# Deformable sampling on one engine: who makes the products, when the distances come, and how long TensorE runs on zeros

## The chip, the cores and the metric

The kernel runs on one core of one Trainium2 chip. The metric is the device time of one execution in microseconds, and a kernel's time is the median of several executions. A core has five engines that run side by side: TensorE (PE in the profile, with its weight loads as PEld), VectorE (DVE), ScalarE (ACT), GpSimd (POOL) and SyncE (SP), which here only issues transfers. They wait for each other through semaphores.

## The reference, cut to what matters

The input x is (8, 32, 16, 16) in fp32. Three layers follow each other, each added to its input: a deformable 3x3 convolution, a state-space scan of 64 states over 256 tokens, and a chain of 33 attention and feed-forward layers in which the data choose which are carried out. Only the first is touched:

```python
x = x + _L0_conv_ref(_gn(x), offset_w, offset_b, weight, bias)

offsets = conv2d(x, offset_w, offset_b, PAD)            # 18 channels: dy, dx of 9 taps
ys = (arange(H) - PAD) + kh + dy
xs = (arange(W) - PAD) + kw + dx
sampled = bilinear_sample(x, ys, xs)                    # (b, tap, y, x, c)
out = einsum('bkhwc,ock->bohw', sampled, w) + bias
```

Bilinear sampling is a weighted sum over all 256 positions of the image: position (i, j) has the weight max(0, 1 - |ys - i|) * max(0, 1 - |xs - j|).

## The kernel before, in words

**Preparation.** x lies as 128 partitions (4 image pairs times 32 channels) by two halves of 256 positions. VectorE normalises it into a zero-padded tile, xpad (L550), and copies it out unpadded (L555). TensorE computes the offsets with nine shifted fp32 matmuls (L803, two passes each in the trace, 18 records), VectorE adds bias and grid (L561), TensorE turns the result so that positions are partitions (L839). Ahead of the nine matmuls stands `keep_warm(12)` (L828): twelve bf16 matmuls of zeros, 128x512, that nobody reads (L824). Beside this TensorE multiplies the image with the nine taps' weights ("filters", L817) in four parts, and ScalarE copies each part out of PSUM in two instructions (`evacuate_filters`, L391).

**The weights of bilinear sampling.** They are made in six rounds, `it` = 0 to 5: three kernel rows times two halves. `distances(it)` on VectorE writes y or x position minus level (L568) and its absolute value (L573), 768 elements a partition. `hats(it)` on ScalarE makes max(0, 1 - that) of it (L398). Then each of the round's three taps, j = 0, 1, 2, needs a product of its row hat and its column hat, `sampling_chunk` (L228): 2048 elements a partition, fp32, both inputs in SBUF and broadcast. There are 18 such chunks. Tile `samp[j]` is one buffer for each j, so the product of round `it` waits until TensorE has turned the chunk of round it - 1 with the same j (L226). VectorE makes j = 0 and 1, GpSimd makes j = 2.

**What TensorE and ScalarE do with a chunk.** TensorE turns a chunk with 16 transposes (`turn`, L860) in two sides of eight. ScalarE copies each side out of PSUM (L415) into `sampT[j]`. TensorE then adds up the tap with 16 matmuls (`tap_sum`, L870) into a PSUM bank that is kept through all 18 chunks. TensorE's order is written out: turn of chunk n, then tap sum of chunk n - 1 (L876 to L880).

**The order of the queues before.** Every engine works off its list in order.

- VectorE: distances 0 and 1, then for each round products j = 0 and 1, then the distances of round it + 2 (L575 to L582).
- GpSimd: some constants (L323 to L333), then the products j = 2 of rounds 0 to 5 (L337), then it waits for the second layer (L340).
- ScalarE: filters 0 and 1, hats 0, filters 2, hats 1, filters 3 (L400 to L405), then for each round the six copies of the turned sides, with the hats of round it + 2 behind those of j = 1 (L417).
- TensorE: the twelve zero matmuls, the offset matmuls, filters, the turn of the offsets, filters (with four zero matmuls in front of parts 2 and 3), then x itself as a matmul with the identity (L846), a wait for all filters (L847), then the 18 chunks.

Behind the last tap sum VectorE adds the bias (L586) and the next layer begins. The state-space layer (L637, L648 and L362 above all) and the chain of layers (from L1009) are not touched.

Of the kernel before, what the change touches and what calls it, by code (L numbers as in the profile page):

```python
# [14 lines left out]
SIDE = 16  # L15
PAIRS, HALVES = 4, 2
# [26 lines left out]
def hybrid_kernel(nc, x, const, offset_w, conv_w, ssm_w, spread_w, masks, steps, w_attn, w_up, w_down, out):  # L43
# [7 lines left out]
    with ctx:  # L51
# [43 lines left out]
        def region(phase, n):  # L95
            a = used[phase]
            used[phase] = a + n
            assert used[phase] <= 31 * 1024
            return pool[:, a:a + n]
# [9 lines left out]
        samp = [region("conv", 8 * HW).rearrange("p (c n) -> p c n", c=8) for _ in range(3)]  # L109
# [45 lines left out]
        def bank(i, n=1):  # L155
            return ps[:, i * BANK:(i + n) * BANK]
# [10 lines left out]
        def slot(e):  # L167
# [10 lines left out]
        off_done, off_ready, offT_done, hat_diff, hat_ready = map(  # L178
            sem, ["off_done", "off_ready", "offT_done", "hat_diff", "hat_ready"])
        z_done, z_ready = map(sem, ["z_done", "z_ready"])  # L180
        samp_made = [sem(f"samp_made{j}") for j in range(3)]
        samp_turned, turned_ready, chunk_summed, conv_done = map(
            sem, ["samp_turned", "turned_ready", "chunk_summed", "conv_done"])
# [33 lines left out]

        ROWS = 3

        def sampling_chunk(eng, it, j):  # L220

            eng.wait_ge(hat_ready, it + 1)

            if it:

                eng.wait_ge(samp_turned, 6 * (it - 1) + 2 * j + 2)  # L226
            now = hat[:, it, :, 2 * j:2 * j + 2, :]
            eng.tensor_tensor(samp[j].rearrange("p c (y x) -> p c y x", y=SIDE),  # L228
                              now[:, :, 0, :].unsqueeze(3).broadcast_to([128, 8, SIDE, SIDE]),
                              now[:, :, 1, :].unsqueeze(2).broadcast_to([128, 8, SIDE, SIDE]),  # L230
                              ALU.mult).then_inc(samp_made[j], 1)

        def column_half(c):
            return slice(c * BANK, (c + 1) * BANK)
# [31 lines left out]
        def _(sp):  # L266
# [19 lines left out]

            regs = control_registers(sp, "sp")
            steps_done, _, _ = counters(sp, "sp")
            layer, op = regs[0], regs[1]
            sp.wait_ge(ctl_ready, 1)  # L290
# [23 lines left out]
        @block.gpsimd  # L314
        def _(pool_e):
            pool_e.memset(ones[:, :], 1.0).then_inc(table_input, 1)
            pool_e.memset(eps[:, :], GN_EPS).then_inc(eps_set, 1)
            pool_e.memset(zero_bf[:, :], 0.0).then_inc(zero_set, 1)  # L318
            pool_e.memset(xpad, 0.0).then_inc(pad_zeroed, 1)
            pool_e.memset(wbd[:, :, :], 0.0).then_inc(wbd_zeroed, 1)  # L320

            pool_e.wait_ge(spread_in, 16)
            pool_e.tensor_copy(picks[:, :].rearrange("p (j b d) -> p b j d", j=PER, b=HALVES),  # L323
                               spread[:, :].rearrange("p (b j) -> p b j", b=HALVES).unsqueeze(3)
                               .broadcast_to([96, HALVES, PER, DI])).then_inc(picks_ready, 1)

            pool_e.wait_ge(const_in, 16)
            onehot = part["onehot"].rearrange("p (b w) -> p b w", b=HALVES)
            pool_e.tensor_copy(chosen[:, 0:2 * PER - 1], onehot[:, 0, :]).then_inc(chosen_ready, 1)  # L330
            pool_e.tensor_copy(chosen[:, 2 * PER - 1:], onehot[:, 1, PER - 1:]).then_inc(chosen_ready, 1)

            pool_e.tensor_copy(row0_picks[:, :].rearrange("p (k d) -> p k d", k=GROUPS * HALVES),  # L333
                               ident.rearrange("p (k j) -> p k j", j=PER)[:, :, 0].unsqueeze(2)
                               .broadcast_to([128, GROUPS * HALVES, DI])).then_inc(row0_picks_ready, 1)

            for it in range(HALVES * ROWS):  # L337
                sampling_chunk(pool_e, it, 2)

            pool_e.wait_ge(c_ready, 1)  # L340

            def product(e):
                j, g = divmod(e, GROUPS)
                if j >= 2:

                    pool_e.wait_ge(prod_summed, j - 1)
                pool_e.wait_ge(scanned, e + 1)
                return prod[GROUPS * (j % 2) + g], state[e % GROUPS]

            def added(j):  # L350
                e = GROUPS * j + GROUPS - 1
                pool_e.wait_ge(delta_copied, j + 1)
                if j:

                    pool_e.wait_ge(scanned, e - GROUPS + 1)
                pool_e.tensor_tensor(dbx[e % GROUPS], bx, delta_wide[j % 2], ALU.mult).then_inc(pool_dbx_ready, 1)  # L356

            pool_e.wait_ge(bx_ready, 1)
            for e in range(DI - 2):
                j, g = divmod(e, GROUPS)  # L360
                to, of = product(e)
                pool_e.tensor_tensor(to, of, cn, ALU.mult).then_inc(prod_ready, 1)  # L362
                if g == 0 and j < PER - 1:
                    added(j)
            to, of = product(DI - 2)
            for c in range(2):
                pool_e.tensor_tensor(to[:, column_half(c)], of[:, column_half(c)], cn[:, column_half(c)],
                                     ALU.mult).then_inc(late_prod_ready, 1)
# [3 lines left out]
        def _(act):  # L372
# [14 lines left out]
            def evacuate_filters(n):  # L387
                half, side = divmod(n, 2)
                for two in range(2):
                    act.wait_ge(z_done, 2 * n + two + 1)  # L390
                    act.activation(zs[:, half, 2 * two:2 * two + 2, side, :], bank(3 + 2 * two, 2)  # L391
                                   .rearrange("p (q k) -> p q k", q=2)[:, :, 0:TAPS * C], ACT.Copy).then_inc(z_ready, 1)

            def hats(i):

                act.wait_ge(hat_abs, i + 1)
                v = hat[:, i, :, :, :].rearrange("p c o y -> p (c o y)")
                act.activation(v, v, ACT.Relu, bias=1.0, scale=-1.0).then_inc(hat_ready, 1)  # L398
# [2 lines left out]
            evacuate_filters(1)  # L401
            hats(0)
            evacuate_filters(2)
            hats(1)
            evacuate_filters(3)  # L405

            for it in range(HALVES * ROWS):
                for j in range(3):
                    if it:

                        act.wait_ge(chunk_summed, 3 * (it - 1) + j + 1)
                    for side in range(2):
                        s = 2 * j + side
                        act.wait_ge(samp_turned, 6 * it + s + 1)
                        act.activation(sampT[j][:, 2 * side:2 * side + 2].rearrange("p q h n -> p (q h n)"),  # L415
                                       bank(2 + 2 * (s % 3), 2), ACT.Copy).then_inc(turned_ready, 1)
                    if j == 1 and it + HALVES < HALVES * ROWS:  # L417
                        hats(it + HALVES)

            def layer_norm(n):
# [30 lines left out]
            for e in range(DI):  # L452
                j, g = divmod(e, GROUPS)
# [72 lines left out]
        def _(dve):  # L526
# [37 lines left out]
            def distances(i):  # L564
                kk, half = divmod(i, HALVES)
                pos = bank(1)[:, half * HW:(half + 1) * HW].rearrange("p (c o) -> p c o", c=8)[:, :, 6 * kk:6 * kk + 6]
                v = hat[:, i, :, :, :]
                dve.tensor_tensor(v, pos.unsqueeze(3).broadcast_to([128, 8, 6, SIDE]),  # L568
                                  part["level"].unsqueeze(1).unsqueeze(1).broadcast_to([128, 8, 6, SIDE]),
                                  ALU.subtract).then_inc(hat_diff, 1)  # L570
                dve.wait_ge(hat_diff, i + 1)
                flat = v.rearrange("p c o y -> p (c o y)")
                dve.scalar_tensor_tensor(flat, flat, -1.0, flat, ALU.mult, ALU.max).then_inc(hat_abs, 1)  # L573

            dve.wait_ge(offT_done, 1)  # L575
            for half in range(HALVES):
                distances(half)
            for it in range(HALVES * ROWS):
                for j in range(2):
                    sampling_chunk(dve, it, j)  # L580
                if it + HALVES < HALVES * ROWS:
                    distances(it + HALVES)  # L582

            dve.wait_ge(conv_done, 1)
# [209 lines left out]
        def _(pe):  # L795
# [25 lines left out]
            def keep_warm(n, at=7):  # L821

                for _ in range(n):
                    pe.matmul(bank(at), zero_bf[:, 0:128], zero_bf[:, :], start=True, stop=True)  # L824

            pe.wait_ge(zero_set, 1)
            keep_warm(12)  # L828
            pe.wait_ge(offw_in, 16)
            pe.wait_ge(xn_ready, HALVES)  # L830
            offset_taps(range(TAPS)).then_inc(off_done, 1)
# [135 lines left out]
            for e in range(DI):  # L967
                spread_delta(e)
                j, g = divmod(e, GROUPS)
# [244 lines left out]
```

## Time and profile before

| | us |
|---|---|
| median of three executions | 369.01 (368.79 to 369.76) |
| the profiled execution | 367.8, its span 366.0 |
| PE busy | 261.8 (72% of the span) |
| DVE busy | 283.0 (77%) |
| ACT busy | 165.2 (45%) |
| POOL busy | 209.7 (57%) |

The span runs from the first to the last instruction; all times inside it are counted from its start. The times in the table are sums over stages with different limits, so the reading below goes by stage.
### The profile page before, as it was taken

What the parts mean: (1) busy time and instruction counts of PE and PEld (TensorE: products, weight loads), DVE (VectorE), ACT (ScalarE), POOL (GpSimd) and SP (SyncE); (2) the same over time, 40 slices, a digit from 0 to 9 for tenths busy, and PEclk for the clock granted to TensorE, in tenths of its full rate; (3) what the DMA queues carried; (4) which work ended last, traced back from release to release, by engine and by line L of the source; (5) the groups of instructions that cost most, each with busy time, mean ns of one, the idle gap of its engine ahead of it and who ended that gap; (6) DMA issues with size and microseconds to landing.
All of it is one profiled execution on the core that took longest, in us unless ns stands there. A gap on an engine that the chain in (4) does not pass through costs nothing. (4 is left out here: it accounts for less than half of the span.)

```text
span 366.0 us, 3919 instructions
## 1 busy us (share of the span) xinstructions
PE 261.8 (72%) x1382; PEld 99.2 (27%) x1388; DVE 283.0 (77%) x223; ACT 165.2 (45%) x263; POOL 209.7 (57%) x98
## 2 busy tenths in 40 slices
PE   5996999997852765477557745775576587788983
PEld 1435777773420000000000000000000143235630
DVE  1179999703589999999999999999999993123731
ACT  1063777662653444344434443444344350334431
POOL 2231444440039999999999999999999850000000
PEclk9898999999996655655565565555565599999999
DMA  6100000000120000000000000000000000000000
GB/s 202 56 0 2 2 0 2 2 3 0 29 58 2 0 0 0 0 1 2 0 0 0 1 0 1 2 0 0 0 0 0 0 2 0 13 18 0 0 0 29
DMA packets 2498, 3.88 MB, mean 11 GB/s; under 512 B 687, under 2 KB 1712, under 8 KB 2480
## 3 DMA queue, kind: packets, MB, share of 16 engines
q1 hardware_dynamic: 2216, 3.45, 3.3%
q8 instruction: 11, 0.18, 0.2%
q10 hardware_dynamic: 264, 0.20, 0.2%
q14 instruction: 7, 0.06, 0.1%
HBM read 2.59 MB, written 0.26 MB: 8 GB/s over the span
## 5 line engine op out<-in xcount | busy, mean ns | idle before, releaser
L362 POOL TENSOR_TENSOR pool<-pool 128x1024 f32<-128x1024 f32 x62 | 144.7, 2355 | 39.3 <-DVE pool L648 39.3
L648 DVE TENSOR_TENSOR_SCAN pool<-ps,pool 128x1024 f32<-128x1024 f32 x63 | 143.8, 2283 | 0.6 <-ACT ps L464 0.5
L957 PE MATMUL ps<-pool,picks 96*128 96x512 bf16 x120 | 59.1, 593 | 72.9 <-DVE pool L648 72.9
L462 ACT ACTIVATE ps<-ps,ssmw 128x1020 f32<-128x1020 f32 x64 | 69.4, 1084 | 74.3 <-DVE pool L637 74.3
L963 PE MATMUL ps<-pool,chosen 128*32 128x512 f32 x256 | 59.4, 1022 | 1.8 <-DVE pool L665 1.8
L637 DVE TENSOR_TENSOR pool<-pool,ps 128x1024 f32<-128x1024 f32 x49 | 58.5, 1195 | 0.8 <-PE ps L938 0.8
L957 PEld LDWEIGHTS ps<-pool,picks 96*128 96x128 bf16 x120 | 7.7, 108 | 146.1 <-DVE pool L648 146.1
L228 POOL TENSOR_TENSOR pool<-pool 128x2048 f32<-128x2048 f32 x6 | 23.6, 3928 | 38.4 <-PE ps L860 29.8
L415 ACT ACTIVATE pool<-ps 128x1024 f32<-128x1024 f32 x36 | 34.9, 1023 | 18.6 <-PE ps L860 18.6
L860 PE MATMUL ps<-cst,pool 128*128 128x128 f32 x288 | 36.5, 282 | 3.8 <-DVE pool L228 3.8
L860 PEld LDWEIGHTS ps<-cst,pool 128*128 128x128 f32 x288 | 32.5, 144 | 11.1 <-issue 11.1
L356 POOL TENSOR_TENSOR pool<-pool 128x1024 f32<-128x1024 f32 x15 | 35.2, 2346 | 0.2 <-ACT pool L450 0.2
L228 DVE TENSOR_TENSOR pool<-pool 128x2048 f32<-128x2048 f32 x12 | 31.3, 2650 | 2.5 <-PE ps L860 2.5
L450 ACT ACTIVATE pool<-ps 128x1024 f32<-128x1024 f32 x15 | 15.4, 1024 | 32.4 <-PE ps L957 29.6
L824 PE MATMUL ps<-zero_bf 128*128 128x512 bf16 x101 | 26.7, 408 | 2.4 <-POOL zero_bf L318 1.4
L870 PE MATMUL ps<-pool 128*32 128x256 f32 x288 | 19.3, 385 | 0.2 <-ACT pool L415 0.2
L824 PEld LDWEIGHTS ps<-zero_bf 128*128 128x128 bf16 x105 | 10.1, 104 | 18.0 <-issue 8.7
L963 PEld LDWEIGHTS ps<-pool,chosen 128*32 128x32 f32 x256 | 6.6, 140 | 28.6 <-issue 27.0
L573 DVE SCALAR_TENSOR_TENSOR pool<-pool 128x768 f32<-128x768 f32 x6 | 13.2, 2208 | 0.2
L803 PE MATMUL ps<-pool,offw 128*128 128x512 f32 x18 | 9.5, 688 | 3.5 <-DVE pool L550 3.5
L464 ACT ACTIVATE ps<-zero_bf 128x4 f32<-128x4 bf16 x64 | 11.2, 175 | 0.0
L497 ACT ACTIVATE pool<-ps,pool 128x256 f32<-128x256 f32 x16 | 7.4, 479 | 6.6 <-DVE pool L751 6.6
(133 smaller groups left out, 196.4 us busy)
## 6 DMA issues: line engine op xcount, KB each, us to landing
ssmw<-ssm_w_dram SPq DMA_DIRECT2D x1, 896.0 KB, 8.8
pool<-pool SPq DMA_DIRECT2D x12, 64.0 KB, 2.0
offw<-offset_w_dram SPq DMA_DIRECT2D x1, 576.0 KB, 6.6
cst<-const_dram SPq DMA_DIRECT2D x1, 426.0 KB, 7.2
xq<-x_dram SPq DMA_DIRECT2D x2, 128.0 KB
convw<-conv_w_dram SPq DMA_DIRECT2D x1, 144.0 KB, 7.1
pool<-w_up_dram SPq DMA_DIRECT2D x2, 64.5 KB
out_dram<-fin SPq DMA_DIRECT2D x1, 128.0 KB
```

The lines of the kernel that those rows point to most:

```text
L228: eng.tensor_tensor(samp[j].rearrange("p c (y x) -> p c y x", y=SIDE), now[:, :, 0, :].unsqueeze(3).broadcast_to([128, 8, SIDE, SIDE]), no ...
L356: pool_e.tensor_tensor(dbx[e % GROUPS], bx, delta_wide[j % 2], ALU.mult).then_inc(pool_dbx_ready, 1)
L362: pool_e.tensor_tensor(to, of, cn, ALU.mult).then_inc(prod_ready, 1)
L415: act.activation(sampT[j][:, 2 * side:2 * side + 2].rearrange("p q h n -> p (q h n)"), bank(2 + 2 * (s % 3), 2), ACT.Copy).then_inc(turned ...
L462: act.activation(decay[:, :, 1:HW], decay[:, :, 1:HW], ACT.Exp, scale=wt["a"][:, PER * g + j:PER * g + j + 1]).then_inc(da_ready, 1)
L637: dve.tensor_tensor(dbx[e % GROUPS], bx, slot(e), ALU.mult).then_inc(dbx_ready, 1)
L648: dve.tensor_tensor_scan(state[e % GROUPS], slot(e), dbx[e % GROUPS], 0.0, ALU.mult, ALU.add)\
L824: pe.matmul(bank(at), zero_bf[:, 0:128], zero_bf[:, :], start=True, stop=True)
L860: ins = pe.transpose(bank(2 + 2 * (s % 3), 2)[:, at:at + 128], samp[j][:, 4 * t + 2 * side + q, hh * 128:hh * 128 + 128], ident)
L870: ins = pe.matmul(bank(0)[quad(q), half * HW:(half + 1) * HW], zs[:, half, q, hh, k * C:(k + 1) * C], sampT[j][:, q, hh, :], start=False, ...
L957: ins = pe.matmul(slot(e)[:, column_half(c)], picks[:, j * 128:(j + 1) * 128], stack[0:96, g * SEQ + c * BANK:g * SEQ + (c + 1) * BANK], s ...
L963: ins = pe.matmul(bank(c)[quad(g), :], chosen[:, PER - 1 - j:3 * PER - 1 - j], prod[GROUPS * (j % 2) + g][:, column_half(c)], start=False, ...
```

## The change

The changed kernel lets VectorE make all three products of each round, and GpSimd none; the distances of round it + 1 are made behind the first product of round `it`, those of round 0 alone before the first product; ScalarE takes hats 1 behind filters 3, and the hats of round it + 1 behind the copies of chunk j = 0 of round `it`; and the first run of zero matmuls has 20 in place of 12.

```diff
-            for it in range(HALVES * ROWS):
-                sampling_chunk(pool_e, it, 2)
-
             pool_e.wait_ge(c_ready, 1)
...
             hats(0)
             evacuate_filters(2)
+            evacuate_filters(3)
             hats(1)
-            evacuate_filters(3)
...
-                    if j == 1 and it + HALVES < HALVES * ROWS:
-                        hats(it + HALVES)
+                    if j == 0 and 0 < it < HALVES * ROWS - 1:
+                        hats(it + 1)
...
             dve.wait_ge(offT_done, 1)
-            for half in range(HALVES):
-                distances(half)
+            distances(0)
             for it in range(HALVES * ROWS):
-                for j in range(2):
+                for j in range(3):
                     sampling_chunk(dve, it, j)
-                if it + HALVES < HALVES * ROWS:
-                    distances(it + HALVES)
+                    if j == 0 and it + 1 < HALVES * ROWS:
+                        distances(it + 1)
...
             pe.wait_ge(zero_set, 1)
-            keep_warm(12)
+            keep_warm(20)
             pe.wait_ge(offw_in, 16)
```

## Rows read from the trace of the kernel before

**Rows 1.** Stretches: length, busy time of PE, PEld, DVE, ACT, POOL, granted clock, DMA.
```profile
6.40:9.80 3.40, 0.14 (x1) 0.00 (x0) 1.82 (x7) 0.30 (x1) 0.00 (x0) 0.98 1.03 371
9.80:13.10 3.30, 3.07 (x4) 1.51 (x5) 0.52 (x2) 0.00 (x0) 0.49 (x1) 0.50 0.20 78
13.10:30.40 17.30, 13.50 (x60) 5.61 (x59) 9.96 (x6) 6.23 (x10) 6.68 (x5) 0.99 0.00 0
30.40:33.80 3.40, 3.04 (x16) 3.08 (x17) 3.37 (x4) 1.03 (x1) 0.00 (x0) 0.53 0.02 5
33.80:84.80 51.00, 50.48 (x563) 37.08 (x562) 36.91 (x17) 36.82 (x39) 19.13 (x5) 1.00 0.01 1
102.00:311.00 209.00, 130.29 (x453) 22.45 (x452) 201.97 (x127) 92.54 (x149) 181.60 (x79) 0.61 0.01 2
...
```

**Rows 2.** Timeline 0 to 20: start, duration, engine, line, what, count, idle before and releaser.
```profile
1.39 5.15 PE L824 MATMUL ps<-zero_bf 128*128 128x512 bf16 x12 [1.39 <-POOL zero_bf L318]
...
10.03 9.48 PE L803 MATMUL ps<-pool,offw 128*128 128x512 f32 x18 [3.49 <-DVE pool L550]
...
11.87 0.34 PEld L803 LDWEIGHTS ps<-pool,offw 128*128 128x128 f32 x1 [0.52 <-issue]
...
12.72 0.34 PEld L803 LDWEIGHTS ps<-pool,offw 128*128 128x128 f32 x1 [0.52 <-issue]
...
18.07 0.19 PEld L803 LDWEIGHTS ps<-pool,offw 128*128 128x128 f32 x1 [0.24 <-issue]
...
18.50 0.19 PEld L803 LDWEIGHTS ps<-pool,offw 128*128 128x128 f32 x1 [0.24 <-issue]
...
19.56 0.75 DVE L561 SCALAR_TENSOR_TENSOR pool<-ps,cst 128x512 f32<-128x512 f32 x1 [9.21 <-PE ps L803]
```

**Rows 3.** Timeline 20 to 37: distances, hats, first products, first turns.
```profile
23.10 0.84 ACT L398 ACTIVATE pool<-pool 128x768 f32<-128x768 f32 x1
...
24.03 4.43 POOL L228 TENSOR_TENSOR pool<-pool 128x2048 f32<-128x2048 f32 x1 [8.68 <-ACT pool L398]
...
24.85 7.96 DVE L228 TENSOR_TENSOR pool<-pool 128x2048 f32<-128x2048 f32 x2
...
25.76 1.19 ACT L391 ACTIVATE pool<-ps 128x576 f32<-128x576 f32 x2
...
25.88 1.12 PE L846 MATMUL ps<-xq,cst 128*128 128x512 f32 x2
...
30.75 5.05 PE L860 MATMUL ps<-cst,pool 128*128 128x128 f32 x32 [3.75 <-DVE pool L228]
...
32.73 0.94 DVE L568 TENSOR_TENSOR pool<-ps,cst 128x768 f32<-128x768 f32 x1
...
34.59 4.49 DVE L228 TENSOR_TENSOR pool<-pool 128x2048 f32<-128x2048 f32 x2
```

**Rows 4.** Timeline 36 to 85: one round of the even pace, and its end.
```profile
39.64 1.97 PE L860 MATMUL ps<-cst,pool 128*128 128x128 f32 x16
...
42.54 1.97 PE L860 MATMUL ps<-cst,pool 128*128 128x128 f32 x16
...
80.24 1.97 PE L860 MATMUL ps<-cst,pool 128*128 128x128 f32 x16
...
84.85 0.75 DVE L586 TENSOR_SCALAR t<-ps,cst 128x512 f32<-128x512 f32 x1 [11.59 <-remote]
```

**Rows 5.** Line L228: count, shortest, median and longest in ns, first and last start.
```profile
L228 DVE TENSOR_TENSOR pool<-pool x12: 2277/2278/5761, 24.8 to 71.0; 128x2048 f32<-128x2048 f32 x12
```

**Rows 6.** Timeline 293 to 314: the gate's matmuls and their copy, and ten zeros.
```profile
293.67 3.72 PE L920 MATMUL ps<-tn,ssmw 128*128 128x256 f32 x16
...
297.43 1.02 ACT L467 ACTIVATE pool<-ps 128x1024 f32<-128x1024 f32 x1 [0.79 <-PE ps L920]
...
300.06 0.68 DVE L671 TENSOR_TENSOR pool<-ps,pool 128x512 f32<-128x512 f32 x1
...
313.44 2.32 PE L824 MATMUL ps<-zero_bf 128*128 128x512 bf16 x10 [0.54 <-issue]
```

More of the change, by code:

```diff
@@ L218, in hybrid_kernel, with sampling_chunk @@
         ROWS = 3
-        def sampling_chunk(eng, it, j):
-            eng.wait_ge(hat_ready, it + 1)
+        def sampling_chunk(dve, it, j):
+            dve.wait_ge(hat_ready, it + 1)
             if it:
-                eng.wait_ge(samp_turned, 6 * (it - 1) + 2 * j + 2)
+                dve.wait_ge(samp_turned, 6 * (it - 1) + 2 * j + 2)
             now = hat[:, it, :, 2 * j:2 * j + 2, :]
-            eng.tensor_tensor(samp[j].rearrange("p c (y x) -> p c y x", y=SIDE),
+            dve.tensor_tensor(samp[j].rearrange("p c (y x) -> p c y x", y=SIDE),
                               now[:, :, 0, :].unsqueeze(3).broadcast_to([128, 8, SIDE, SIDE]),
```

## The prediction

> **What bounds the kernel now.** I read the busy time by stretches first, then the timeline from 0 to 85, then the waits of line L228, and the two later stages only to see that nothing there is touched. Up to 84.8 the first layer runs; 209 us of state-space scan follow, in which VectorE is busy for 201.97 [rows 1], and then the chain of layers. Neither is changed. What the change does to the time it must do before 84.8, and what it gains there the rest should pass on: the later stages wait for the layer before, not for a transfer.
>
> In the first layer three pieces differ. Up to 10.03 TensorE waits for the padded input. Its offset matmuls then hold everything up for 9.48 us, and VectorE's L561 is waiting for them [rows 2]. From 20 to 31 the first products are on the path: TensorE stands still for 3.75 us for a product of VectorE [rows 3]. From 36.7 on TensorE is the bound: turns start every 2.90 us (39.64, 42.54, ... 80.24), and over 33.8 to 84.8 it is busy for 50.48 of 51.00 us, where VectorE has 36.91 and ScalarE 36.82 [rows 1, 4]. So a faster producer gains nothing in the even pace. A gain can only come from an earlier start of that pace, and a loss only from a producer that falls behind 3 x 2.90 = 8.70 us a round.
>
> **Eight more zeros.** The twelve zeros take 5.15 us, 0.43 each; ten in the last stage take 2.32, 0.23 each [rows 2, 6]. So the first twelve ran at 1.2 GHz (the records of the clock only begin at 6.43). The records then show 2.4 GHz in 6.4 to 9.8, a stretch in which TensorE did 0.14 us of work, and 1.2 GHz in 9.8 to 13.1, just when the offset matmuls start [rows 1]. The engine had worked for 5.15 us when the clock rose and had been idle for 3.3 when it fell. At 1.2 GHz the weight loads of L803 are 0.85 apart (11.87, 12.72), later 0.43 (18.07, 18.50) [rows 2]. With zeros until the input is there the clock should be at 2.4 GHz throughout: 18 x 0.43 = 7.74 instead of 9.48, a gain of 1.7 us. Can eight more zeros be late? At least 8 x 0.23 = 1.9 us, at most 8 x 0.43 = 3.4 are added to the end at 6.54: they end between 8.4 and 9.96, and the offset matmuls start at 10.03. Either way not late; I take the early end, as the clock rose as the twelfth ended, and at worst the hand-over costs 0.1.
>
> The early end leaves TensorE idle for 1.6 us. The Trainium skill (TensorE: Matmul & The Clock Gate, "What's actually happening") lets the clock fall only after a stretch without work, so by it the 1.7 us are safe. The trace is less kind: in the scan TensorE is busy for 130 of 209 us, yet the mean grant is 0.61 [rows 1]. Both ends therefore stand: 0 if the clock falls before the offset matmuls in spite of the zeros, 1.7 if not. I take 1.7: an idle time of 1.6 us is nearer to the short pauses of 13.1 to 30.4 (busy for 13.50 of 17.30, grant 0.99) than to the 3.3 us of nothing after which it fell.
>
> **One distance first, and no GpSimd product.** I work in the times of before and take the 1.7 off at the end. Hats 0 end at 23.94; GpSimd's first product starts at 24.03, VectorE's only at 24.85, behind distances 1. VectorE's first lasts 5.76 us [rows 3, 5], while GpSimd works until 28.46; alone a product lasts 2.28, and two take 34.59 to 38.99, 2.20 apiece. (38.99 is where distances of the next round start; 4.49 is the printed busy time.) 5.76 less the wait until 28.46 (3.61) leaves 2.15: the product waited for GpSimd's to end.
>
> After the change, in VectorE's order: product 0 from 24.0 to 26.2; distances 1, which take 1.86 (32.73 to 34.59 [rows 3]), to 28.1; product 1 to 30.3; product 2 to 32.5. GpSimd's removed products leave nothing behind: its next wait is far later.
>
> ScalarE: filters 3 are copied one hats instruction (0.84) earlier at best, 25.4 to 26.6; hats 1 then wait for distances 1 and run from 28.1 to 28.95. The copies of the first turned chunk are queued behind this wait. The first turn can start at 27.0, when L846 ends [rows 3], so its first side is ready at 28 and waits 1 us; copies of both sides end at 30.9. Who waits for them is the tap sum of chunk 0, which comes behind the turn of chunk 1 (30.35 to 32.3). So that wait is covered by 1.4 us. Tap sum 0 runs to 33.3, and turn 2, whose product was ready at 32.5, starts at 33.3. Before, the turns 0 and 1 ran 30.75 to 35.8 at 1.2 GHz in part (grant 0.53 [rows 1]), a tap sum of 1.0 followed, and turn 2 started at 36.74, which is 15 x 2.90 = 43.5 before the last turn at 80.24 [rows 4]. Gain 36.74 - 33.3 = 3.4 us. It supposes 2.4 GHz in turn 1: idle time before it is 1.35 us in place of 3.75. At 1.2 GHz turn 1 would cost 1 us more.
>
> **The even pace.** VectorE's round is 3 x 2.20 + 1.86 = 8.46, TensorE's is 8.70. Product 4 is ready at 30.3 + 8.46 = 38.8, turn 4 begins at 33.3 + 5.8 = 39.1, and the margin grows by 0.24 a round. The later hats follow the copies of chunk j = 0: turn start + 2.0 + 1.0 + 0.85, some 4.0 us behind the turn; the product and the distances that need them have 8.7 until the next j = 0 turn, so product j = 0 (4.0 + 2.2) is ready 2.5 us early, and product j = 1 (1.86 + 2.2 later) 1.3 us. ScalarE has as many instructions as before. Everything from 36.74 is thus moved as it is.
>
> For this step the Trainium skill offers a rule against the change: Perfetto Trace Analysis, "Optimizing Scalar/DVE Operations", says that offloading to GpSimd may make sense where VectorE is saturated, and adds that between these two it might not help. By the first half the even pace would suffer, and the second rival below is what it would look like.
>
> **The sum.** 1.7 + 3.4 = 5.1, say 5.0 for waits between engines that I have counted as nothing. The profiled execution gives 367.8 - 5.0 = 362.8; it stands 1.2 us under the median of 369.01, which gives 364.0.
>
> **The rivals.**
>
> - *The clock falls before the offset matmuls all the same.* For it: the scan's grant of 0.61 with TensorE busy for 62%. Against: the stretches of rows 1 up to 33.8 as read above. Only 3.4 - 0.1 remain: 365.7. Chance 0.15.
> - *VectorE becomes the bound by a little.* If the products stand 2.28 apart plus 0.1 of handing over each, a round is 3 x 2.38 + 1.96 = 9.1; five rounds of 0.4 more than TensorE's, less the lead of 0.3, cost 1.7: 365.7. For it: a margin of only 0.24 us in 8.7. Against: the pair 34.59 to 38.99, measured with ScalarE and TensorE at work. Chance 0.07.
> - *The clock of the later stages moves.* The gate's matmuls ran at 2.4 GHz in 3.72 us, as the clock rose just before them, and their copy ended at 298.45, where its reader came at 300.06 [rows 6]. With an unlucky clock they take 3.7 more, of which 1.6 are hidden: + 2.1, 366.1. Before and after can both draw this; the three executions lie 1.0 apart. Chance 0.07, and as much of the same size the other way is in the forecast's range.
> - *The product alone is slower than its rows say.* This is the one that ends slower: all 18 lie on VectorE, and were another user of its operands than GpSimd to blame for 5.76, each could cost more than 2.2. Shifted by the 1.7, products start at 22.3, so the last ends at 22.3 + 18p + 5 x 1.86, and the last turn must start no later than 80.24: no gain is left from p = 2.70. At 2.9, between the median and the 5.76, the end is 83.8, so 3.6 later: 372.6. Against it stand the median of 2.28 for twelve and the fit of 5.76 with GpSimd's end. Chance 0.03.
> - *It doesn't start earlier*, say because ScalarE's wait for distances 1 holds back more than I see, and the clock falls too: within 0.3% of before, 369. Chance 0.03.
>
> The forecast itself has 0.65. A difference of about 0.3%, 1.1 us, is what a measurement of this kernel can tell from none. Faster by more: 0.65 + 0.15 + 0.07 + 0.07 = 0.94. The range takes in the first three rivals above, 366.3, and below the case that the executions of before pay more for the clock at 10 and at 31 than the profiled one did (1.7 less): 362.3.
>
> **What would show it.** TensorE: 20 zeros that end by 8.5 to 10; 18 offset matmuls in 7.7 to 7.9 us and the grant at 1.00 over them; L561 near 17.9. VectorE: first product at about 22.3, lasting 2.3; products of 2.20 to 2.28 throughout, GpSimd with none. Turns start every 2.90 from turn 2 at about 31.7; L586 at 79.8 in place of 84.85; scan and chain of layers as long as before. Wrong would be: a grant of 0.5 over L803 (first rival), idle time of TensorE before L860 in later rounds, released by L228 (second or fourth), a tail that is longer than before with the same instructions (third).

## The result and the profile after

The changed kernel takes 363.78 us, the median of four executions (362.57 to 364.62), against 368.9 us before; the ratio is 0.9869 with a 95% interval of 0.9838 to 0.9899. That is 1.3% or some 5 us faster. Of all the executions below five fell in a slower state of the chip (one of the kernel before, two each of two variants), and medians and ratios leave them out. The profiled execution has 363.64 us and a span of 361.9, 4.1 less than before. Lines behind the edits stand three lower in the changed kernel: L857 is the turn, L867 the tap sum, L800 the offset matmuls, L821 the zeros, L583 the bias at the end of the first layer. Turn n and product n are those of chunk n, counted from 0.

The timeline of the changed kernel up to the fourth turn (start, duration, engine, line, what, count, idle before and releaser); it answers to [rows 2] and [rows 3]:

```profile
1.39 7.24 PE L821 MATMUL ps<-zero_bf 128*128 128x512 bf16 x20 [1.39 <-POOL zero_bf L318]
...
10.10 7.97 PE L800 MATMUL ps<-pool,offw 128*128 128x512 f32 x18 [1.47 <-DVE pool L547]
...
18.10 0.75 DVE L558 SCALAR_TENSOR_TENSOR pool<-ps,cst 128x512 f32<-128x512 f32 x1 [7.69 <-PE ps L800]
...
22.52 2.29 DVE L228 TENSOR_TENSOR pool<-pool 128x2048 f32<-128x2048 f32 x1 [0.91 <-ACT pool L395]
...
26.59 6.69 DVE L228 TENSOR_TENSOR pool<-pool 128x2048 f32<-128x2048 f32 x3
26.71 0.84 ACT L395 ACTIVATE pool<-pool 128x768 f32<-128x768 f32 x1 [1.36 <-DVE pool L570]
...
28.94 1.97 PE L857 MATMUL ps<-cst,pool 128*128 128x128 f32 x16 [1.56 <-DVE pool L228]
...
31.84 1.97 PE L857 MATMUL ps<-cst,pool 128*128 128x128 f32 x16
...
37.64 1.73 PEld L857 LDWEIGHTS ps<-cst,pool 128*128 128x128 f32 x16 [0.41 <-DVE pool L228]
```

The 20 zeros end at 8.63, TensorE is idle for 1.47 us, and the offset matmuls take 7.97 us where they took 9.48. The first product lasts 2.29 instead of 5.76. Turn 2 starts at 31.84 (before 36.74). Turns then come every 2.90 us, and turn 4 at 37.64 has its product just in time.

The end of the first layer, answering to [rows 4]:

```profile
75.34 1.97 PE L857 MATMUL ps<-cst,pool 128*128 128x128 f32 x16
...
79.95 0.75 DVE L583 TENSOR_SCALAR t<-ps,cst 128x512 f32<-128x512 f32 x1 [8.40 <-remote]
```

31.84 to 75.34 are the same 43.5 us as 36.74 to 80.24 before. The layer ends 4.90 earlier. The products, in the view of their line, answering to [rows 5]:

```profile
L228 DVE TENSOR_TENSOR pool<-pool x18: 2281/2284/2292, 22.5 to 69.3; 128x2048 f32<-128x2048 f32 x18
```

And the stretches, answering to [rows 1] (length, busy PE, PEld, DVE, ACT, POOL, granted clock, DMA):

```profile
9.80:13.10 3.30, 3.00 (x7) 1.43 (x8) 0.58 (x2) 0.00 (x0) 0.45 (x1) 1.00 0.15 60
...
30.40:80.00 49.60, 48.98 (x549) 35.58 (x548) 41.06 (x25) 35.57 (x38) 0.00 (x0) 1.00 0.01 2
...
97.00:306.00 209.00, 131.31 (x453) 22.94 (x453) 202.07 (x127) 92.47 (x149) 181.51 (x79) 0.60 0.01 3
```

The scan's 209 us are as before. The granted clock stays at 1.00 from the records' first entry to the end of the layer: neither the fall at 9.8 nor the one at 30.4 is there. Of the 4.90 us, 0.75 are given back behind the scan in this execution. The down projection in the first pass of the chain of layers (L1107, at 314.67) takes 3.35 us instead of 2.78, while the clock is at 1.2 GHz (granted clock 0.53 over 314.6 to 317.8), which is 0.57 of them; the rest goes just before it, where TensorE waits for a transfer.

### The profile page after: what moved, and what is told of

Same layout as the page of the kernel before. It is cut to its first block and busy times, and to the rows that moved or that the text cites. A ratio compares the mean times of both kernels' runs of the same rounds, so it can differ in the third digit from the quotient of the medians.

```text
span 361.9 us, 3935 instructions
## 1 busy us (share of the span) xinstructions
PE 262.7 (73%) x1390; PEld 98.7 (27%) x1396; DVE 284.2 (79%) x229; ACT 165.3 (46%) x263; POOL 186.1 (51%) x92
## 3 DMA queue, kind: packets, MB, share of 16 engines
q1 hardware_dynamic: 2216, 3.45, 3.3%
## 5 line engine op out<-in xcount | busy, mean ns | idle before, releaser
L228 DVE TENSOR_TENSOR pool<-pool 128x2048 f32<-128x2048 f32 x18 | 40.1, 2285 | 0.9 <-ACT pool L395 0.9
L857 PE MATMUL ps<-cst,pool 128*128 128x128 f32 x288 | 35.4, 275 | 1.6 <-DVE pool L228 1.6
L857 PEld LDWEIGHTS ps<-cst,pool 128*128 128x128 f32 x288 | 31.2, 140 | 9.1 <-issue 6.2
L821 PE MATMUL ps<-zero_bf 128*128 128x512 bf16 x109 | 28.8, 410 | 2.7 <-POOL zero_bf L318 1.4
L867 PE MATMUL ps<-pool 128*32 128x256 f32 x288 | 19.3, 385 | 0.2 <-ACT pool L412 0.2
L821 PEld LDWEIGHTS ps<-zero_bf 128*128 128x128 bf16 x113 | 11.0, 105 | 20.4 <-issue 10.4
L960 PEld LDWEIGHTS ps<-pool,chosen 128*32 128x32 f32 x256 | 6.7, 140 | 27.6 <-issue 25.9
L388 ACT ACTIVATE pool<-ps 128x576 f32<-128x576 f32 x8 | 4.8, 648 | 10.7 <-PE ps L814 10.7
L867 PEld LDWEIGHTS ps<-pool 128*32 128x32 f32 x288 | 7.5, 109 | 6.6 <-issue 2.9
L800 PE MATMUL ps<-pool,offw 128*128 128x512 f32 x18 | 8.0, 596 | 1.5 <-DVE pool L547 1.5
```

The lines of the kernel that those rows point to most:

```text
L228: dve.tensor_tensor(samp[j].rearrange("p c (y x) -> p c y x", y=SIDE), now[:, :, 0, :].unsqueeze(3).broadcast_to([128, 8, SIDE, SIDE]), no ...
L857: ins = pe.transpose(bank(2 + 2 * (s % 3), 2)[:, at:at + 128], samp[j][:, 4 * t + 2 * side + q, hh * 128:hh * 128 + 128], ident)
L867: ins = pe.matmul(bank(0)[quad(q), half * HW:(half + 1) * HW], zs[:, half, q, hh, k * C:(k + 1) * C], sampT[j][:, q, hh, :], start=False, ...
L960: ins = pe.matmul(bank(c)[quad(g), :], chosen[:, PER - 1 - j:3 * PER - 1 - j], prod[GROUPS * (j % 2) + g][:, column_half(c)], start=False, ...
```

## The experiments

The time of one execution moves by 1 us and more for reasons treated at the end. So each run is read in two ways: as a median with its ratio to the kernel before, and from its profile as the time from the start of the offset matmuls to the bias at the end of the layer (before: 10.03 to 84.85 = 74.82; changed: 10.10 to 79.95 = 69.85). This second figure leaves out when the input lands, but it is read from one execution, and holds the clock that this execution happened to get. Line numbers differ a little from run to run: the turn is L857, L858 or L860, the product L228 or L229.

**One part at a time.** Four kernels ran on one chip, beside the kernel before (369.07 us). The first has only the zeros:

```diff
-            keep_warm(12)
+            keep_warm(20)
```

> The kernel before with 20 zero matmuls in place of 12 and nothing else. Theory: the clock is at 2.4 GHz over the offset matmuls, they take 8.0 us instead of 9.48, L561 starts near 18.1, everything behind it 1.4 to 1.7 us earlier, but the first turns still stand behind 5.76 us of contended product and run partly at 1.2 GHz. Time 1.5 us under the kernel before. Rival (the clock falls again before the offset matmuls): no gain. Rival (the gain needs the other edits): no gain.

Measured: 367.41 us, ratio 0.9961 (0.9933 to 0.9990). Its timeline:

```profile
10.14 7.97 PE L803 MATMUL ps<-pool,offw 128*128 128x512 f32 x18 [1.51 <-DVE pool L550]
...
29.35 6.10 PE L860 MATMUL ps<-cst,pool 128*128 128x128 f32 x32 [3.75 <-DVE pool L228]
...
36.38 1.97 PE L860 MATMUL ps<-cst,pool 128*128 128x128 f32 x16
```

The offset matmuls gain 1.5 us as expected, but turns 0 and 1, which start 1.40 earlier, now take 6.10 us instead of 5.05: they come behind the same 3.75 us of idle time, and more of them falls into the stretch at 1.2 GHz. Here the clock was at 1.2 GHz from 27.5 to 34.4 (granted clock 0.50 over 27.6 to 34.3), in the kernel before from 30.3 to 33.7. Turn 2 starts only 0.36 earlier, and offset matmuls to bias take 74.35, 0.47 less than before. So in this execution most of what the zeros gained was lost at the next pause. The medians do not say the same: they are 1.66 us apart, the 1.5 that were expected. The profile of the kernel before was a fast one, 1.2 us under its median, and with one profile of each kernel the loss at the pause is seen, but its usual size is not.

The second has the changed order and products, but 12 zeros:

```diff
-            keep_warm(20)
+            keep_warm(12)
```

> The changed kernel with 12 zero matmuls, so the new order and VectorE's products alone. Theory: turn 2 starts 3.4 us before the kernel before's 36.74, at 33.3 to 33.5, the pace behind it is 2.90, time 3.3 us under the kernel before and 1.5 us over the changed kernel. Rival (the parts are not additive, since the clock at the first turns depends on the zeros): turn 2 at 34.3 or later, and only 2.3 us under the kernel before.

Measured: 366.36 us, ratio 0.9919 (0.9891 to 0.9947). Offset matmuls 9.84 to 19.5 (9.67 us), turn 2 at 33.27, bias at 81.39: 71.55, which is 3.27 less than before and 1.70 more than the changed kernel. Turn 2 and the layer are as the first theory had them; the time is 2.7 us under the kernel before, between theory and rival. By these profiles the parts are not additive: 0.47 and 3.27 alone, 4.97 together. Of the 1.23 us between, 1.04 are the clock at the first turns of the run with zeros only, and 0.19 are the 9.67 us here against 9.48 before, with 12 zeros both. By the medians they nearly are: 1.66 and 2.71 alone, 4.7 to 5.1 together, with intervals of about 1 us to either side of each. Whether the parts add up is therefore not settled.

The third keeps the old order of distances and hats, with 20 zeros and all products on VectorE:

```diff
-            distances(0)
+            for half in range(HALVES):
+                distances(half)
             for it in range(HALVES * ROWS):
                 for j in range(3):
                     sampling_chunk(dve, it, j)
-                    if j == 0 and it + 1 < HALVES * ROWS:
-                        distances(it + 1)
+                if it + HALVES < HALVES * ROWS:
+                    distances(it + HALVES)
```

ScalarE's hats stand where they stood in the kernel before as well.

> 20 zeros and all products on VectorE, but distances and hats in the order of the kernel before (distances 0 and 1 first, those of round it + 2 behind round it). Theory of mine, that GpSimd's product was what held VectorE up and the order of the distances is not needed: product 0 starts at 23.4, 0.9 later than in the changed kernel, but product 1 is ready at 27.8 in place of 28.9, turn 2 starts near 30.7 to 31.0 in place of 31.84, and the time is equal or up to 0.9 us less than the changed kernel. Rival, that distances one round ahead earn what the words of the change suggest: the time is 1 us or more above the changed kernel.

Measured: 363.48 us, ratio 0.9876 (0.9828 to 0.9924), as fast as the changed kernel. Against the run with zeros only it differs in nothing but who makes the products: 3.9 us less by the medians, 5.03 less from offset matmuls to bias. This is the larger part of the gain. Its timeline:

```profile
23.30 6.69 DVE L228 TENSOR_TENSOR pool<-pool 128x2048 f32<-128x2048 f32 x3
...
27.84 1.98 PE L858 MATMUL ps<-cst,pool 128*128 128x128 f32 x16 [0.17 <-DVE pool L228]
...
30.75 1.97 PE L858 MATMUL ps<-cst,pool 128*128 128x128 f32 x16
...
34.10 1.97 PE L858 MATMUL ps<-cst,pool 128*128 128x128 f32 x16 [0.38 <-DVE pool L228]
```

Turn 2 starts at 30.75, 1.1 earlier than in the changed kernel, then turn 3 waits for a product that stands behind distances 2. 10.00 to 79.32 are 69.32 us, 0.53 less than the changed kernel. So the distances one round ahead bring nothing once VectorE makes all products.

The fourth gives GpSimd its third of the products back and keeps the rest:

```diff
             for it in range(HALVES * ROWS):
-                for j in range(3):
+                for j in range(2):
                     sampling_chunk(dve, it, j)
...
+            for it in range(HALVES * ROWS):
+                sampling_chunk(pool_e, it, 2)
```

> The changed kernel, but GpSimd makes product j = 2 of each round as before. Theory (GpSimd's product and VectorE's instructions with two SBUF inputs keep each other out at the start): VectorE's second product ends between 31.5 and 33 in place of 28.9, turn 2 starts 2.7 to 4.3 us later than in the changed kernel, time 2.7 to 4.3 us over it. Rival (order and clock are the whole gain, the engine does not matter): same time as the changed kernel.

Measured: 373.26 us, ratio 1.0134 (1.0090 to 1.0178), so slower than the kernel before, and by more than either theory had. Its timeline, first the start, then round 2:

```profile
22.45 2.29 DVE L228 TENSOR_TENSOR pool<-pool 128x2048 f32<-128x2048 f32 x1 [0.91 <-ACT pool L398]
22.50 5.78 POOL L228 TENSOR_TENSOR pool<-pool 128x2048 f32<-128x2048 f32 x1 [7.18 <-ACT pool L398]
...
25.64 3.45 DVE L573 SCALAR_TENSOR_TENSOR pool<-pool 128x768 f32<-128x768 f32 x1
...
31.35 3.68 PE L860 MATMUL ps<-cst,pool 128*128 128x128 f32 x16 [4.05 <-DVE pool L228]
...
43.42 2.29 DVE L228 TENSOR_TENSOR pool<-pool 128x2048 f32<-128x2048 f32 x1 [5.86 <-ACT pool L398]
...
47.44 3.68 POOL L228 TENSOR_TENSOR pool<-pool 128x2048 f32<-128x2048 f32 x1 [5.01 <-PE ps L860]
47.49 7.98 DVE L228 TENSOR_TENSOR pool<-pool 128x2048 f32<-128x2048 f32 x2
...
53.32 3.62 PE L860 MATMUL ps<-cst,pool 128*128 128x128 f32 x16 [2.13 <-DVE pool L228]
...
74.57 1.98 PE L860 MATMUL ps<-cst,pool 128*128 128x128 f32 x16 [2.13 <-DVE pool L228]
```

Whoever comes second waits for the whole of the other's instruction. VectorE's product starts 0.05 us before GpSimd's, keeps its 2.29, and GpSimd's then takes 5.78 instead of 3.68. GpSimd in turn stretches VectorE's L573 from 0.96 to 3.45. I had reckoned with that at the start only. From round 2 on the new order makes it worse: with only one round of lead VectorE waits 5.86 us for hats 2, which ScalarE makes behind its copies of a chunk, and so its second product meets GpSimd's at 47.4 and TensorE waits again. Offset matmuls to bias: 10.02 to 90.79, 80.77 us. With GpSimd's products the new order is 5.8 us slower than the old one with as many zeros (367.41). The Trainium skill (SBUF — State Buffer, "SBUF: two separate sides") calls the port pair that GpSimd shares with VectorE instructions of two SBUF inputs an exclusive lock, which the one who starts first holds for its whole instruction; this trace agrees with its 5.78 and 3.45.

**Zeros and margins.** Four further kernels, beside the kernel before (368.10 us). With 28 zeros:

```diff
-            keep_warm(20)
+            keep_warm(28)
```

> The changed kernel with 28 zero matmuls in place of 20. In the changed kernel the 20 end at 8.63 and the input is there at 10.10, so 1.5 us are empty. Theory: eight more at 0.23 end at 10.5, the offset matmuls start 0.3 to 0.4 late, the clock stays at 2.4 GHz as it did over the gap, and everything behind moves by that: 0.3 us slower. Rival (the gap still costs clock in some executions): equal or faster by up to 1 us.

Measured: 363.02 us, ratio 0.9847 (0.9796 to 0.9898). The zeros ended at 9.65, not at 10.5, because the clock rose at 5.5 in this execution and at 7.3 in that of the changed kernel; the offset matmuls started on time, took 7.97, and the layer took 69.85, as with 20. So 28 cost nothing here, against my expectation.

With two more VectorE instructions behind each of the five later distances:

```diff
                         distances(it + 1)
+                        for n in range(2):
+                            dve.tensor_tensor(extra[:, 2 * it + n, :], xq[:, :], xq[:, :], ALU.mult)
```

> The changed kernel with two more VectorE instructions (512 columns each, some 0.55 us) behind each of the five later distances; their results are not used. It measures the margin of VectorE behind TensorE. Theory (VectorE 8.46 us a round, TensorE 8.70): 1.1 us more makes VectorE the bound at 9.55 a round; its last product, which ends at 71.5 in the changed kernel, ends at 77, the last turn starts there in place of 75.34, and TensorE's idle time before L857 released by L228 grows in every round. Time 1.3 to 1.9 us over the changed kernel. Rival (VectorE still has slack): same time.

Measured: 367.79 us, ratio 0.9986 (0.9957 to 1.0015), some 4 us over the changed kernel where 1.3 to 1.9 were expected. The direction is right, the size is not: offset matmuls to bias take 74.95, 5.1 more than in the changed kernel. The pair costs 1.21 us, and one pair stands ahead of product 1. That moved the start, which I had left out, and turn 1, behind the longer pause, ran partly at 1.2 GHz. Its timeline:

```profile
29.72 3.11 PE L860 MATMUL ps<-cst,pool 128*128 128x128 f32 x16 [2.77 <-DVE pool L229]
...
34.23 1.97 PE L860 MATMUL ps<-cst,pool 128*128 128x128 f32 x16
...
58.74 1.97 PE L860 MATMUL ps<-cst,pool 128*128 128x128 f32 x16 [0.91 <-DVE pool L229]
```

From the start of the offset matmuls turn 2 is 2.8 us later than in the changed kernel (24.56 against 21.74), and the even pace adds 2.3.

With distances 0 and 1 first, and the later ones behind the second product:

```diff
-            distances(0)
+            for half in range(HALVES):
+                distances(half)
             for it in range(HALVES * ROWS):
                 for j in range(3):
                     sampling_chunk(dve, it, j)
-                    if j == 0 and it + 1 < HALVES * ROWS:
+                    if j == 1 and 0 < it < HALVES * ROWS - 1:
                         distances(it + 1)
```

ScalarE takes hats 1 ahead of filters 3 again; the later hats stay behind the copies of chunk j = 0.

> 20 zeros, all products on VectorE, distances 0 and 1 both before the first product, and those of round it + 1 behind the second product of round it, from round 1 on. In the run with the old order, turn 2 started at 30.75 but turn 3 waited 0.38 for product 3, which stood behind distances 2. Theory: product 3 is ready at 32.1, no turn behind turn 1 waits for VectorE, turns start every 2.90 from 30.75, L586 at 78.9 in place of 79.95 (changed kernel) and 79.32 (old order). Time 1.0 us under the changed kernel. Rival (ScalarE's wait for the later distances holds back its copies): time equal to the changed kernel or over it.

Measured: 362.90 us, ratio 0.9841 (0.9803 to 0.9880), 0.8 us under the changed kernel by the medians, with intervals that overlap. No turn waits for VectorE behind turn 1, but the timeline of this profile shows what 20 zeros do not always prevent:

```profile
1.39 5.79 PE L822 MATMUL ps<-zero_bf 128*128 128x512 bf16 x20 [1.39 <-POOL zero_bf L318]
9.81 9.67 PE L801 MATMUL ps<-pool,offw 128*128 128x512 f32 x18 [2.63 <-DVE pool L547]
```

The clock rose earlier, the zeros ended at 7.18, the pause was 2.63 us, and the clock fell at 10.6, under the offset matmuls. So the time from there, 70.54, holds 1.70 of clock; without it, it would be 68.84, an estimate.

Without zeros (`keep_warm(0)`):

> The changed kernel without the first zero matmuls. Theory: the offset matmuls start at the same time, 10.1, at 1.2 GHz, and take 9.5 to 9.7 us as behind 12 zeros (9.67), so 12 zeros bought nothing: time 1.4 to 1.7 us over the changed kernel, the same as with 12. Rival (the twelve bought a part): 2.5 us or more over it.

Measured: 364.13 us, ratio 0.9894 (0.9837 to 0.9950). The offset matmuls take 9.53 us and the layer 71.41, near the 71.55 with 12 zeros: in the layer the twelve bought nothing. The median lies only 0.35 over the changed kernel's, where 1.4 to 1.7 were expected, and 2.2 under that with 12 zeros, whose interval overlaps. The input landed at 6.79 in this profile, and between 7.10 and 7.64 in the thirteen with zeros; whether that comes of the missing zeros or of chance was not tried.

**The last four**, beside the kernel before (368.33 us). The changed kernel again:

> The changed kernel as it is, as the measure for the three beside it. 363.8 as on record, within 1 us.

Measured: 363.66 us, ratio 0.9870 (0.9842 to 0.9897), and again 69.85 from offset matmuls to bias.

The late distances with 28 zeros:

> The order of the run with two distances first and the later ones behind the second product, with 28 zeros. In that run's profile the 20 zeros ended at 7.18, the clock fell at 10.6 and the offset matmuls took 9.67 us. Theory: the order is worth 1.0 us and the longer row of zeros removes the executions with a slow start: offset matmuls 7.97 us, turn 2 at 30.8 to 31.0, L586 at 78.9 to 79.1, time 1.0 to 1.5 us under the changed kernel run beside it. Rival (both only move waits): same time as the changed kernel.

Measured: 362.98 us, ratio 0.9847 (0.9819 to 0.9875). In the first layer the expectation holds; its timeline:

```profile
10.08 7.92 PE L801 MATMUL ps<-pool,offw 128*128 128x512 f32 x18
...
30.78 1.97 PE L858 MATMUL ps<-cst,pool 128*128 128x128 f32 x16
...
78.89 0.75 DVE L584 TENSOR_SCALAR t<-ps,cst 128x512 f32<-128x512 f32 x1 [8.40 <-PE ps L879]
```

10.08 to 78.89 are 68.81 us, 1.04 less than the changed kernel. The medians differ by 0.7, and the intervals overlap, so as a time the gain is not settled.

The margin of the even pace alone, with one extra instruction in rounds 2 to 5:

```diff
                         distances(it + 1)
+                        if it:
+                            dve.tensor_tensor(extra[:, it, :], xq[:, :], xq[:, :], ALU.mult)
```

> The changed kernel with one more VectorE instruction (512 columns, 0.60 us by the run with two of them) behind the distances of rounds 2 to 5 each, so that the start stays as it is and only the even pace is tried. Product (it, 1) is ready 0.4 us ahead of its turn in round 1 of the changed kernel, and the lead grows by 0.24 a round. Theory: VectorE's round is 9.06, the turns j = 1 wait 0.2, then 0.36 more a round, L586 1.3 us later (81.3), time 1.3 us over the changed kernel. Rival (product's end and turn are not that tight): under 0.4 us.

Measured: 364.43 us, ratio 0.9891 (0.9865 to 0.9918). The instruction adds 0.60 us, and four turns, all of them j = 1, wait for it; the timeline has the first two:

```profile
37.69 1.97 PE L860 MATMUL ps<-cst,pool 128*128 128x128 f32 x16 [0.30 <-DVE pool L229]
...
46.76 1.98 PE L860 MATMUL ps<-cst,pool 128*128 128x128 f32 x16 [0.30 <-DVE pool L229]
```

46.76 - 37.69 = 9.07 in this timeline: that is VectorE's round of 8.46 plus 0.60. The layer takes 71.33, 1.48 more, and the median is 0.8 higher. So a round of 8.46 is safe by 0.24 us and no more.

GpSimd from round 1 on, in the old order with 20 zeros:

```diff
-            for it in range(HALVES * ROWS):
+            for it in range(1, HALVES * ROWS):
                 sampling_chunk(pool_e, it, 2)
...
-                for j in range(2):
+                for j in range(2 if it else 3):
                     sampling_chunk(dve, it, j)
```

> The kernel before with 20 zeros, where VectorE makes all three products of round 0 and GpSimd the third product from round 1 on. Theory: the start is that of the run with the old order (product 1 ready at 27.8, turn 2 near 30.75), but GpSimd's product of round 1 now may start at 32.7, when turn 2 is over, waits for VectorE's product 3 to end at 34.0 and keeps product 4 out until 37.7; turn 4 waits until 39.9 in place of 37.0, so L586 near 82.2 and the time 2 to 3 us over the changed kernel. Rival (only the first product of GpSimd ever hurt): L586 near 79.3 and the time at or under the changed kernel.

Measured: 367.01 us, ratio 0.9955 (0.9929 to 0.9980), 3.4 over the changed kernel. Its timeline:

```profile
30.60 1.97 PE L860 MATMUL ps<-cst,pool 128*128 128x128 f32 x16
...
31.63 7.97 DVE L228 TENSOR_TENSOR pool<-pool 128x2048 f32<-128x2048 f32 x2
...
32.73 4.73 POOL L228 TENSOR_TENSOR pool<-pool 128x2048 f32<-128x2048 f32 x1 [17.61 <-ACT pool L398]
...
39.66 3.49 PE L860 MATMUL ps<-cst,pool 128*128 128x128 f32 x16 [2.72 <-DVE pool L228]
```

The start is as in the run with the old order, turn 2 at 30.60. Then GpSimd keeps product 4 out until 37.46, and turn 4 starts at 39.66. The pause costs the clock too: the turn takes 3.49 us, and turn 5 starts 4.42 behind it, at 44.08. From there the pace is 2.90, and offset matmuls to bias take 73.62, 3.77 more than in the changed kernel. Removing GpSimd's first product alone only moves the collision on.

## Why the prediction was right, and where it was not

**The total.** 364.0 was forecast, 363.78 measured, in the range, and the case was the one given 0.65. That the two lie 0.2 us apart is luck in part. The profiled execution was to take 362.8 and took 363.64, since 0.75 us were given back in the chain of layers; and the 1.2 us added for the distance from profile to median turned out to be 0.14.

**Eight more zeros.** The zeros ended at 8.63, between my 8.4 and 9.96, and were not late. The offset matmuls gained 1.51 in place of 1.7: 7.97 us. They do start 0.43 apart, so the 18th starts 7.31 behind the first, but it ends 0.66 later and not 0.43. In the changed order the row of zeros is worth 1.70 from offset matmuls to bias, beside 12 zeros at 9.67. But the step was added to the next as if it stood by itself. In the profile of the zeros alone it was worth 0.47, since the clock stayed down longer at the next pause; by the medians 1.66. The sum came out with both edits made; what it would have been worth for one of them alone, the prediction could not have said.

**The rule on the clock.** My first rival, priced at 1.7 with chance 0.15, is real: of the nine profiles with 20 zeros one (two distances first) shows the clock fall under the offset matmuls, behind a pause of 2.63 us; in the other eight the pauses were up to 2.22 and it stayed at 2.4 GHz. How long the pause is depends on when the clock rises during the zeros, as they end the sooner for it: at 3.8 in the profile that fell, at 5.1 to 7.3 in the others. The Trainium skill (TensorE: Matmul & The Clock Gate, "What's actually happening") says that the point of change is not tied to the start of the kernel and varies from run to run, and so it does here. The length of a pause alone does not decide: with a third of the products on GpSimd two turns came behind a pause of 2.13 us each, and the one at 53.32 took 3.62 us (granted clock 0.51 over 53.6 to 56.9), the one at 74.57 only 1.98 (1.00).

**One distance first, no GpSimd product.** By my times less 1.7: product 0 at 22.3 (measured 22.52), turn 1 at 28.65 (28.94), turn 2 at 31.6 (31.84). ScalarE waited 1.36 us for distances 1, covered as worked out. The cause of the 5.76 was read rightly: with the same order and zeros, taking the products from GpSimd is worth 3.9 us, and the two runs that gave it some back show the same wait again. The trace of before also shows what takes part in it:

```profile
38.86 3.76 POOL L228 TENSOR_TENSOR pool<-pool 128x2048 f32<-128x2048 f32 x1 [10.40 <-PE ps L860]
38.99 0.95 DVE L568 TENSOR_TENSOR pool<-ps,cst 128x768 f32<-128x768 f32 x1
...
39.98 3.46 DVE L573 SCALAR_TENSOR_TENSOR pool<-pool 128x768 f32<-128x768 f32 x1
```

L568, one of whose two inputs lies in PSUM, takes its usual 0.95 us while GpSimd works; L573, with both in SBUF, takes 3.46 instead of 0.96. There it cost nothing, as TensorE was the bound.

What I did not do was to take the two edits apart: I priced them together and never asked what the order was worth. The runs say: the products moved to VectorE bring the gain, and the distances one round ahead take 0.5 us of it back in the first layer, as they put product 1 behind distances 1; the medians do not tell the two orders apart.

**The even pace.** VectorE's 8.46 against 8.70 held to 0.01: product 4 ready 0.3 us early in the forecast, turn 4 with no more than its usual 0.41 of PEld idle in the profile, and the run with 0.60 more per round makes VectorE the bound at 9.07. Of the Trainium skill's advice (Perfetto Trace Analysis, "Optimizing Scalar/DVE Operations"), that offloading to GpSimd may make sense where VectorE is saturated and that between these two it might not help, the second half is borne out here: with a third on GpSimd the kernel is 3.9 us slower in the old order, and 9.6 in the new one, where VectorE is busy for 8.46 of 8.70 us a round.

**The later stages.** Moved as they are, but for 0.75 us of the 4.90 in the profiled execution. 0.57 of them are the clock, which is the kind of my third rival, but not its 2.1 us, and at another place: the down projection and not the gate. The other 0.18 stand at a wait for a transfer, which the prediction had ruled out for these stages.

**The slower rival** stayed out: products lasted 2.28 to 2.29, all 18 of them.

## What to carry to other kernels

Before sharing elementwise work out between VectorE and GpSimd, look for a VectorE instruction that lasts a multiple of its median: where both read two operands from SBUF, the one that comes second waits for all of the other's, and a product of 2.28 us on VectorE beats 3.7 us beside it. Then compare the producer's round with the consumer's; a margin of 3% was enough here, and 0.6 us more was not. And where an edit gains time ahead of a pause, look at the clock behind the pause: in one profile here it took away 1 us of 1.5. How often it does cannot be told from one profile.

## What the runs showed of the hardware that I had not expected

A single execution can differ by more than 4 us for the clock alone. The profiled execution of the late distances with 28 zeros took 367.44 us, where the median of its six is 362.98, though its first layer was the shortest of all. Its stretches in the attention step:

```profile
317.30:334.30 17.00, 14.66 (x71) 8.49 (x70) 5.09 (x10) 7.10 (x21) 0.00 (x0) 1.00 0.04 9
334.40:344.50 10.10, 10.10 (x35) 6.18 (x35) 4.33 (x6) 3.18 (x13) 0.00 (x0) 0.50 0.00 0
344.60:358.00 13.40, 11.38 (x71) 5.23 (x68) 5.96 (x16) 5.09 (x11) 0.00 (x0) 1.00 0.00 0
```

And of its timeline:

```profile
336.08 1.97 PE L1053 MATMUL ps<-cst,pool 128*128 128x128 f32 x8
```

The same eight transposes take 1.10 us at 2.4 GHz in the profile of the changed kernel. For 10 us of the attention step TensorE ran at 1.2 GHz, busy all the while, behind a stretch in which it had been busy for 14.66 of 17.00 us. From the first of these transposes to the down projection behind them this execution took 23.64 us (332.36 to 356.00), the changed kernel's 18.73 (333.32 to 352.05): the 4.9 us between are more than the 3.8 by which its span is longer (365.7 against 361.9).

Two other profiles show a shorter fall at the same step, that of the old order with all products on VectorE (granted clock 0.51 over 330.1 to 333.4) and that of two distances first (0.54 over 331.5 to 334.8); in the changed kernel's there was none. Why the clock falls there in some executions stays open. What can be carried off is that a stage's length, read from the profile, told changes of half a microsecond apart that medians of the whole kernel did not, as long as the granted clock of the stage was the same in both.
